# Second mixture, shared part: the search round placed behind the first split of a pair, and the ordering of two experts in four later pieces

## The reference, cut to what matters

```python
z = xf @ proj_w.T + proj_b                         # 2048 tokens x 8 experts
s = sigmoid(z) + expert_bias
probs = softmax(log(clip(s, 1e-12)))
topk_w, topk_idx = top_k(probs, 2)                 # two experts for each token
topk_w = topk_w / topk_w.sum(-1)
pair_e, pair_w, pair_tok = ...                     # 4096 pairs of a token and an expert
cap = 640                                          # most pairs that an expert keeps
kept_w, kept_pair = top_k(where(assigned, pair_w, -inf), cap)   # the 640 heaviest of each expert
xe = xf[kept_tok]
h = gelu(xe @ fc1_w + fc1_b);  oe = h @ fc2_w + fc2_b
y = zeros.at[kept_tok].add(oe * kept_w)
sh = gelu(xf @ sh1_w.T + sh1_b) @ sh2_w.T + sh2_b  # the shared part: every token, 1024 hidden
return sh + y
```

## Time and profile before

| what | us |
|---|---|
| three timed runs: lowest, median, highest | 1092.89, 1094.52, 5164.06 |
| span of the profiled execution | 1091.8 |
| TensorE busy in it | 960.8 (88%) |
| VectorE busy in it | 771.6 (71%) |
| ScalarE busy in it | 613.0 (56%) |
| GpSimd busy in it | 237.9 (22%) |

### The profile page before, as it was taken

How to read it: one execution, slowest core, us unless ns; L and a number is a source line. 1 busy time by engine, 2 the same in 40 slices (tenths; PEclk the granted TensorE clock), 3 DMA queues, 4 the chain that set the end, 5 groups by cost and what they waited for, 6 DMA issues and landing times. The chain is left out here.

```text
span 1091.8 us, 23012 instructions
## 1 busy us (share of the span) xinstructions
PE 960.8 (88%) x8426; PEld 897.9 (82%) x8426; DVE 771.6 (71%) x1924; ACT 613.0 (56%) x1460; POOL 237.9 (22%) x307
## 2 busy tenths in 40 slices
PE   3699999877798769999999999999979899899991
PEld 2588888667687648989999999999979899899991
DVE  5777787667576668878676777776776777566655
ACT  3476667348597645555555555555547345476750
POOL 3434343203200342010101100000000000557731
PEclk9899999878898879999999999999998999999996
DMA  8321111001355220000000000003006000444517
GB/s 260 119 96 61 41 60 41 1 1 45 109 176 127 70 68 1 20 1 20 2 20 20 1 20 2 21 1 98 1 2 194 1 1 1 110 142 146 146 49 260
DMA packets 66031, 69.70 MB, mean 64 GB/s; under 512 B 14337, under 2 KB 56833, under 8 KB 65793
## 3 DMA queue, kind: packets, MB, share of 16 engines
q1 hardware_dynamic: 59424, 53.28, 16.0%
q0 software_dynamic: 5376, 14.69, 4.6%
q10 hardware_dynamic: 1120, 0.27, 0.1%
HBM read 46.20 MB, written 22.02 MB: 62 GB/s over the span
## 5 line engine op out<-in xcount | busy, mean ns | idle before, releaser
L1439 PE MATMUL a_psK<-a_kvThi,a_wk 128*128 128x512 f32 x256 | 97.5, 422 | 4.9 <-DVE a_klo L1643 3.5
L307 POOL TENSOR_SCALAR t_neg<-t_raw,t_nthr 128x256 bf16<-128x256 f32 (+1 forms) x54 | 60.7, 1138 | 109.9 <-DVE t_nthr L498 109.9
L1498 PE MATMUL a_psY<-a_nwhi,a_uhi 128*128 128x256 f32 x256 | 73.8, 288 | 5.1 <-DVE a_ulo L1671 5.1
L1558 ACT ACTIVATE a_probs<-a_psS,a_softmax 128x256 f32<-128x256 f32 x128 | 59.6, 471 | 30.4 <-DVE a_softmax L1653 30.4
L1479 PE MATMUL a_psU<-a_pThi,a_tokhi 128*128 128x256 f32 x256 | 72.4, 283 | 0.0
L1479 PE MATMUL a_psU<-a_pTlo,a_tokhi 128*128 128x256 f32 x256 | 72.4, 283 | 0.0
L1479 PE MATMUL a_psU<-a_pThi,a_toklo 128*128 128x256 f32 x256 | 72.4, 283 | 0.0
L1548 ACT ACTIVATE a_khi<-a_psK,a_bk 128x512 fp32r<-128x512 f32 x64 | 44.1, 688 | 50.3 <-PE a_psK L1439 50.2
L1498 PE MATMUL a_psY<-a_nwlo,a_uhi 128*128 128x256 f32 x256 | 72.2, 282 | 0.0
L1498 PE MATMUL a_psY<-a_nwhi,a_ulo 128*128 128x256 f32 x256 | 72.1, 282 | 0.0
L1611 POOL TENSOR_TENSOR a_toklo<-a_kv,a_tokhi 128x512 fp32r<-128x512 f32 x16 | 22.0, 1378 | 227.9 <-ACT a_tokhi L1543 227.9
(11 more groups left out here) (385 smaller groups left out, 3237.9 us busy)
## 6 DMA issues: line engine op xcount, KB each, us to landing
t_raw<-in_L_ffn_expert_w SPq DMA_DIRECT2D x16, 512.0 KB, 3.8
f_raw<-in_fc_T SPq DMA_DIRECT2D x16, 512.0 KB, 4.9
m_results<-a_zeros SPq DMA_DIRECT2D x8, 512.0 KB, 3.5
m_sorted<-m_zeros SPq DMA_DIRECT2D x1, 3072.0 KB, 12.7
e_xin<-m_sorted SPq DMA_DIRECT2D x24, 128.0 KB, 2.4
m_expert_out<-e_y SPq DMA_DIRECT2D x24, 128.0 KB, 1.7
a_rawkv<-in_L_xattn_Wkv SPq DMA_DIRECT2D x2, 1024.0 KB, 6.0
m_n<-in_sh_T SPq DMA_DIRECT2D x2, 1024.0 KB, 7.7
```

The source lines that it names most:

```text
L307: ins = pool.tensor_scalar(neg[:, own], raw[h % NRAW][:, own], nthr[h % 2][:, n:n + 1], None, ALU.is_lt)
L1439: ins = pe.matmul(psK[:].rearrange("p b t -> p (b t)"), wk[x][:, a, h * DH:(h + 1) * DH], kvT[pair % 2][y][:, a, :, :, :].rearrange("p b m ...
L1498: ins = pe.matmul(psY[:, b, :], u[ch % 2][x][:, f, hh * P:(hh + 1) * P], nw[y][:, f, 2 * j + hh, :], start=first, stop=last, skip_group_ch ...
L1558: act.activation(probs[n % 2][:, b, :], psS[n % 2][:, b, :], ACT.Exp, bias=nmax[:, n % NM, b:b + 1], accum_out=sums[:, n % NM, b:b + 1]).t ...
```

## The change

In `top2()` the split of the fourth group of pair 0 is put between the 16 MAX8 and the 16 searches for the places; it stood behind `count_above` before. In a loop step, VectorE's slot 0 comes behind the first split instead of the second, and its slot 1 behind the third instead of the fourth. `order()` becomes `order(part)` with four parts, which run in steps 1 and 2, each ahead of a `keep`. TensorE's, ScalarE's, GpSimd's and SyncE's lists are the same, and so are VectorE's instructions apart from their order.

```diff
--- before.py
+++ after.py
@@ -2266,6 +2266,7 @@
                     for i in range(NB):
                         ins = dve.max(best[:, i, :], sg[:, i, :])
                     k.step(ins)
+                    split(0, 3)
                     for i in range(NB):
                         ins = dve.max_index(place[:, i, :], best[:, i, :], sg[:, i, :])
                     k.step(ins)
@@ -2283,15 +2284,18 @@
                     k.step(dve.tensor_tensor(wmat[:], wmat[:], tmp[:], ALU.add))
                     k.step(dve.tensor_copy(wT[:], wmat[:].rearrange("p b e -> p e b")))
 
-                def order():
-                    for n, op in enumerate((ALU.min, ALU.max)):
-                        ins = dve.tensor_tensor(ordered[:, n, :], which[:, 0, :], which[:, 1, :], op)
+                def order(part):
+                    if part == 0:
+                        for n, op in enumerate((ALU.min, ALU.max)):
+                            ins = dve.tensor_tensor(ordered[:, n, :], which[:, 0, :], which[:, 1, :], op)
+                    elif part == 1:
+                        for n in range(2):
+                            ins = dve.tensor_tensor(hots[:, n], by_token(ordered[:, n, :]), by_expert(iota[:]), ALU.is_equal)
+                    elif part == 2:
+                        ins = dve.tensor_tensor(own[:], hots[:], wmat[:].unsqueeze(1).to_broadcast([P, 2, NB, NE]), ALU.mult)
+                    else:
+                        ins = dve.tensor_reduce(ws[:], own[:], AX.X, ALU.add)
                     k.step(ins)
-                    for n in range(2):
-                        ins = dve.tensor_tensor(hots[:, n], by_token(ordered[:, n, :]), by_expert(iota[:]), ALU.is_equal)
-                    k.step(ins)
-                    k.step(dve.tensor_tensor(own[:], hots[:], wmat[:].unsqueeze(1).to_broadcast([P, 2, NB, NE]), ALU.mult))
-                    k.step(dve.tensor_reduce(ws[:], own[:], AX.X, ALU.add))
 
                 def count_above(what):
                     k.step(dve.tensor_tensor(above[:], wT[:].unsqueeze(1).to_broadcast([P, CANDS, NE, NB]),
@@ -2443,19 +2447,20 @@
                 top2()
                 dve.wait_ge(s["bits_done"], 1)
                 count_above(bits_of(0))
-                split(0, 3)
-                order()
                 for i in range(PAIRS):
                     more = i + 1 < PAIRS
                     if more:
                         split(i + 1, 0)
-                        split(i + 1, 1)
                     aside(i, 0)
                     if more:
+                        split(i + 1, 1)
                         split(i + 1, 2)
-                        split(i + 1, 3)
                     for j in range(2):
                         aside(i, j + 1)
+                        if more and j == 0:
+                            split(i + 1, 3)
+                        if i in (1, 2):
+                            order((i - 1) * 2 + j)
                         keep(i, j)
                         if not more:
                             if j == 0:
```

## The result

Eleven timed runs of each kernel: 1095.31 us before and 1089.21 us after in the median, ratio 0.9956 with a 95% interval of 0.9939 to 0.9972, that is 4.8 us less (3.1 to 6.7). The two medians themselves lie 6.1 us apart, inside that interval. Forecast were 1089.3 us, between 1086.3 and 1092.2. The profiled span is 1087.3 us against 1091.8.

A forecast was written before the change was run, and what follows sets the result against it. TensorE's waits, set at the front by a chain through top2's searches, a split and a gelu, were taken as the bound. Terms -0.8 - 3.8 - 1.3 = -5.9, plus 1.5 clock: 1091.8 - 4.4 + 1.9 = 1089.3 us, range 1086.3 to 1092.2.

The forecast's parts named there:

- low clock in step 1: TensorE's ups of step 1, after a 3.1 us gap, run at 1.2 GHz: 1.5 us lost, bounds 0 and 3.35.
- the stretch: From the start of the 48 ups beside top2 to step 6's first down: 91.82 us before, 4.4 us less forecast.
- Part 1 and 2: Front: split in top2 turns TensorE's 3.97 us wait into 1.9; split and ordering leave the loop's front, -0.8 us.
- Part 3: Steps 1 to 3: with the search round behind the first split TensorE no longer waits, 3 x 1.27 = -3.8 us.
- The slack of 0.2 to 0.35 us: Slots 2 and 3 of steps 1 and 2: counts come 0.2 to 0.35 us ahead of TensorE.
- rival 2: Rounds' slack of 0.2 to 0.3 us is absent, four slots a step miss: 1093.1 us, chance 0.12.
- Part 4: Steps 4 to 6: marks come 1.4 us earlier and a 0.60 us wait in step 5 goes, -1.3 us.
- Rival 1: The clock holds after the front gaps, so the gain is 5.9 us: 1087.8 us, chance 0.25.
- Rival 4: Ups and downs of step 1: low clock outlasts that step, losing 7.1 us against 5.9: 1095.0 us, chance 0.03.
- Rival 5: Front: split(0, 3) makes nothing earlier, VectorE's 0.9 us wait costs what the ordering saves: 1090.1 us, chance 0.05.
- Rival 3: Experts' part: gain given back by a transfer that doesn't start earlier, 1092 to 1093.7 us, chance 0.05.
- The offset of 1.9 us from span to time: Added to the profiled span to get the median: mean of 1.1 and 2.7 us from two timed runs.

The follow-up runs named there:

- no_split: Changed kernel with split(0, 3) put back behind count_above, ordering and rounds as changed; stretch 85.98 us, ratio 0.9956.
- round_alone: Kernel before with only the search round moved behind the first split of a step; stretch 86.62 us, ratio 0.9967.
- fill: Changed kernel plus 22 matmuls that nobody reads in TensorE's gap ahead of round 1; stretch 86.71 us, ratio 0.9939.
- fill_both: Changed kernel plus unread matmuls in both front gaps, 16 ahead of round 0 and 22 ahead of round 1; stretch 85.95 us, ratio 0.9933.
- interleaved: Changed kernel with split(0, 3) behind the searches, split(1, 0) inside top2, split(1, 1) behind the first count, raise_bar(0) before split(1, 2); stretch 82.23 us, ratios 0.9922, 0.9938.

## Why the prediction was right

Times are from the start of the 48 ups.

| step of the prediction | forecast | measured |
|---|---|---|
| VectorE's wait ahead of the split | 0.9 us | 1.04 us |
| round 0's matmul | 10.8 | 10.93 |
| round 1's matmul | 17.3 | 17.36 |
| low clock in step 1 | 1.5 us | 1.5 us (4.69 us from round 1 to round 2, 3.17 before) |
| a step | 12.3 us | 12.38 us |
| the stretch | 87.4 us | 87.36 us |

**Part 1 and 2**, that the visible wait of 4.0 us would for the most part come back as waits for counts, held: it is what the two rows of L1992 show. Round 1 came 0.73 us earlier than before, 0.8 forecast. The sum priced the two together, and so did not show what no_split does: that the move of the split wins 0.14 us and brings the low clock with it. **Part 3** held: from round 2 to round 14 it is 37.06 us instead of 40.81, 3.75 us less where 3.8 was forecast, and round_alone has it without the rest. The slack of 0.2 to 0.35 us was enough in every slot, so rival 2 did not come about. **Part 4** held: neither the marks nor the spread are waited for, and from round 14 to the first down of step 6 it is 28.25 us instead of 29.75, 1.5 us less where 1.3 was forecast.

One step of the working was wrong although its result was right. I had TensorE idle 3.1 us ahead of round 1 and took that gap as the reason for the low clock. It idled 1.58 us there, because the gap of 2.19 us ahead of round 0 had already been followed by the low level, and down(0, 1) took 4.61 us. That the price in step 1 came out at 1.5 us all the same is partly luck: it was a choice between 1.0 and 1.7, made for another gap than the one that came. That idle time at the front is the cause is shown by fill and fill_both.

**Rival 1**, the clock holds, did not come about: gaps of 2.19 and 1.58 us, with one low piece in between, were each followed by 1.2 GHz. The Trainium skill, page "TensorE: Matmul & The Clock Gate", section "HAM oscillation — how this bites in real kernels", gives as its abstract rule to leave no idle gap of TensorE above a certain length, and both gaps here are shorter than that. By that rule the clock would have stayed up; this trace does not agree. **Rival 4**, a low clock that outlasts step 1, is out: the low piece in it was over after 3.4 us. **Rival 5**, the move and the ordering together make nothing earlier, is out by the 0.73 us of round 1. **Rival 3**, the gain is given back in the experts' part, is not fully settled. On the chips of the experiments the time from the first down of step 6 to the first matmul of an expert is 20.9 to 21.2 us in all twelve runs, whether the stretch ahead of it took 95.2 or 82.0 us: that wait moves along with its cause. In the first pair of profiles it was 0.68 us longer after the change, with a wait of 1.95 us for gathered rows where there had been 1.61, and the clock fell once more behind it. One execution of each can't tell that from scatter.

That the total came out 0.1 us from the forecast is luck beyond the sum. The forecast starts from 1091.8 + 1.9 = 1093.7 us for the kernel before, and its eleven runs had a median of 1095.31; the medians differ by 6.1 us where the sum has 4.4. Two more things outside the sum cancelled. TensorE entered the stretch 1.14 us earlier, which is no effect of the change, and that about made up for the 1.1 us lost behind the stretch. The offset of 1.9 us from span to time, a mean of two values, was 1.8 us in the profiled run after (1089.06 against 1087.3).

## What to carry to other kernels

A long wait that the profile names is worth what is left when the next link of the chain is walked: here 4.0 us of wait held nothing to gain, because the count behind it was no earlier, and moving the split alone made the stretch 3.4 us longer. Put an instruction that must wait for another engine behind the work that is ready, not ahead of it, and let the slower chain start early: the splits that feed ScalarE belong inside VectorE's long serial piece, as in `interleaved`. When a change leaves TensorE idle in pieces of 2 us, count the work behind each piece at both clock levels, and ask whether it is hidden.

## What the runs showed of the hardware that I had not expected

The clock fell behind gaps of 2.19 and 1.58 us, while one of 1.22 us (interleaved, 1.00 from 856.0 to 866.0) was not followed by the low level. Replacing the idle time by matmuls that nobody reads gave back 1.4 us of 87.4.

On the chips of the experiments one stretch at the head of the experts' part was 4.6 us longer than in the first two profiles (20.9 against 16.3 us). In the changed kernel's second profile it holds one wait of 6 us:

```profile
949.00 0.48 DVE L2224 SCALAR_TENSOR_TENSOR x_sb<-f_psY,gates,x_sb 128x256 f32<-128x256 f32 x1 [7.96 <-remote]
949.04 0.66 ACT L2118 ACTIVATE m_turned<-f_psX 128x256 fp32r<-128x256 f32 x2 [7.50 <-remote]
...
950.02 0.66 PE L2038 MATMUL f_psX<-ident,rows 128*128 128x128 f32 x2 [5.99 <-DVE m_turned L2425]
```

VectorE and ScalarE stand still together for 7.5 to 8 us, although down(7, 1), for which that keep waits, had been finished by about 942.9. What held them is not settled; a wait of 6.0 to 6.5 us stands there in all twelve runs, so it enters no comparison among them. The kernel before was not profiled on these chips.
